# GpSimd waits for its cell scatters: a wait at every fourth scatter of a batch

## The reference

```python
loop = jnp.arange(n_nodes, dtype=edge_index.dtype)
row = jnp.concatenate([edge_index[0], loop])
col = jnp.concatenate([edge_index[1], loop])
deg = jax.ops.segment_sum(jnp.ones_like(col, dtype=jnp.float32), col, num_segments=n_nodes)
dinv = jnp.where(deg > 0, jax.lax.rsqrt(deg), 0.0)
norm = dinv[row] * dinv[col]
...
h = h @ W.T
msg = h[row] * norm[:, None]
out = jax.ops.segment_sum(msg, col, num_segments=n_nodes)
```

## The kernel before

| batch | block | scatters |
|---|---|---|
| 1 | end of attention, sums turned back tile by tile (`tiles`, line 1177) | 42 |
| 2 | normalize n1 | 17 |
| 3, 4, 5 | router of the two-expert layer, its choice, its weight loads | 6, 6, 9 |
| 6 | the two experts (`two_experts`, line 1972) | 135 |
| 7, 8 | normalize n2, n3 | 32, 24 |
| (none) | sum over edges: GpSimd gathers 416 tiles of rows | |
| 9, 10 | end of the sum, choice of the six-expert layer | 54, 5 |
| 11 | dispatch of rows to experts | 30 |
| singles | expert tiles: one before every second tile (line 2228) | 28 calls of one |
| 12 | collecting the expert rows (line 2419) | the last 28 |

## Time and profile before

### The profile page before, as it was taken

One profiled execution on the slowest core, in us unless ns is written; L12 is line 12 of the kernel. 1 busy time (PEld: TensorE's weight loads), 2 busy tenths in 40 slices (PEclk: granted clock), 3 DMA queues, 4 the chain that ended last, 5 costly groups with the idle time before them and its releaser, 6 DMA issues. The chain is left out here.

```text
span 5143.9 us, 62246 instructions
## 1 busy us (share of the span) xinstructions
PE 3848.2 (75%) x19117; PEld 2836.3 (55%) x19117; DVE 2174.4 (42%) x6089; ACT 1234.4 (24%) x3514; POOL 1935.0 (38%) x2021
## 2 busy tenths in 40 slices
PE   3877777234735555458399999996969999999597
PEld 2555555112425444357366665654538887777586
DVE  5555556600344444242300000005237777777723
ACT  3555454200100000012200000001125554444332
POOL 3455453474266666445400000001224444444053
PEclk8778888566866766668699999997579999999598
DMA  6655553000023333036454444443434444444266
GB/s 213 175 148 141 150 152 107 1 19 1 3 83 91 92 89 91 25 112 184 143 153 142 142 136 141 140 133 99 113 126 137 134 137 135 133 130 129 69 218 208
DMA packets 424073, 613.62 MB, mean 119 GB/s; under 512 B 149273, under 2 KB 287650, under 8 KB 423490
## 3 DMA queue, kind: packets, MB, share of 16 engines
q1 hardware_dynamic: 310578, 327.46, 22.2%
q0 software_dynamic: 104112, 273.76, 18.6%
q10 hardware_dynamic: 9056, 8.43, 0.5%
HBM read 517.83 MB, written 91.59 MB: 118 GB/s over the span
## 5 line engine op out<-in xcount | busy, mean ns | idle before, releaser
L2217 POOL DMA_INDIRECT stage<-t_row,f_take x168 | 162.1, 965 | 1269.7 <-POOLq L2064 1152.3
L865 POOL DMA_INDIRECT eg_rows<-t_edge,src_i x416 | 393.5, 946 | 563.7 <-DVE eg_pre L1698 422.1
L1108 PE MATMUL ps<-sum_hot,sum_rows 128*128 128x128 f32 x1664 | 330.0, 364 | 365.6 <-issue 201.5
L1372 PE MATMUL ps<-cv_cells,xn 128*128 128x384 f32 (+2 forms) x1600 | 535.7, 493 | 67.2 <-DMA cv_cells<-t_cells 67.2
L271 POOL DMA_INDIRECT t_cells<-times_seen,cell x416 | 409.8, 985 | 413.0 <-PEq L312 152.8
L865 POOL DMA_INDIRECT ag_rows<-t_att,src_i x416 | 401.7, 966 | 386.7 <-DVE ag_msg L970 264.6
L1108 PEld LDWEIGHTS ps<-sum_hot,sum_rows 128*128 128x128 f32 x1664 | 292.7, 264 | 403.0 <-issue 392.9
L865 POOL DMA_INDIRECT sum_rows<-t_row,src_i x416 | 393.9, 947 | 211.3 <-issue 116.5
L1050 PE MATMUL ps<-featT,ag_msg 128*128 128x128 f32 x1664 | 370.7, 357 | 127.2 <-issue 124.4
L1372 PEld LDWEIGHTS ps<-cv_cells,xn 128*128 128x128 f32 x1600 | 304.2, 190 | 279.5 <-DMA cv_cells<-t_cells 67.6
L1650 PE MATMUL ps<-eg_w,eg_rT 128*128 128x256 f32 x1664 | 439.3, 386 | 1.1 <-ACT eg_rT L1668 1.1
(11 more groups left out here) (418 smaller groups left out, 6296.4 us busy)
## 6 DMA issues: line engine op xcount, KB each, us to landing
cv_cells<-t_cells SPq DMA_DIRECT2D x225, 384.0 KB
cv_cells<-t_cells SPq DMA_DIRECT2D x75, 448.0 KB
xn<-in_L_ffn_W SPq DMA_DIRECT2D x57, 512.0 KB
t_cells<-zeros SPq DMA_DIRECT2D x17, 1664.0 KB
xn<-in_L_ffn_expert_w SPq DMA_DIRECT2D x110, 256.0 KB
ag_trow<-t_dst SPq DMA_DIRECT2D x104, 256.0 KB
t_cells<-zeros POOLq DMA_DIRECT2D x8, 1664.0 KB
eg_eaT<-in_edge_attr SPq DMA_DIRECT2D x208, 64.0 KB
```

What stands on the lines that cost most here:

```text
L865: nc.gpsimd.indirect_dma_start(out=rows[:, j, :], out_offset=None, in_=table, in_offset=bass.IndirectOffsetOnAxis(ap=src_i[:, n:n + 1], ax ...
L1108: mm = nc.tensor.matmul(ps[:, j % BANKS, k * EC:(k + 1) * EC], lhs, hot[:, j, :], start=True, stop=True)
L1372: mm = nc.tensor.matmul(ps[:, bank(q, k, half), 0:at.stop - at.start], source(l)[:, s, k * 128:(k + 1) * 128], cells[:, n % CR, at], start ...
L2217: nc.gpsimd.indirect_dma_start(out=xd[:, j, :], out_offset=None, in_=t_row, in_offset=bass.IndirectOffsetOnAxis(ap=take_row[:, n:n + 1], a ...
```

## The change

At every fourth scatter of a batch (offset 0, 4, 8, ... from the batch's first) GpSimd waits until `counted` stands at 16 for each scatter issued so far in the program. `seen[0]` is only raised at the end of a call, so the offsets start anew with each batch, and each of the 28 single calls has its one scatter at offset 0. Scatter 0 keeps its own two waits. Nothing else is changed; SUM_COUNTS, line 50, and the batches keep their sizes.

```diff
@@ -48,6 +48,7 @@
 EARLY_CLEARS = 8
 YR = 5
 SUM_COUNTS = 54
+PACE = 4
 
 
 class Signal:
@@ -268,6 +269,8 @@
             if c == 0:
                 pool.wait_ge(counted.sem, counted.at(0))
                 pool.wait_ge(g.cleared.sem, g.cleared.at(0))
+            elif (c - seen[0]) % PACE == 0:
+                pool.wait_ge(counted.sem, counted.at(16 * c))
             nc.gpsimd.indirect_dma_start(out=t_cells, out_offset=bass.IndirectOffsetOnAxis(ap=cell[:, c:c + 1], axis=0),
                                          in_=times_seen[:, c:c + 1], in_offset=None).then_inc(counted.sem, 16)
         seen[0] = min(RUN, seen[0] + many)
```

## The result

The changed kernel takes 4503.61 us (median of 4 runs, 4493.12 to 4532.5) beside 4390.77 us of the kernel before (4 runs, 4388.14 to 4394.56): ratio 1.0266, 95% interval 1.0236 to 1.0295. It is slower by 112.8 us; forecast were 84, in a range of 40 to 125. This holds for the chip that it was timed on.

The account below looks back on a forecast made before the run. Block by block, GpSimd arriving last at most scatter batches' ends was taken to bound the kernel. 84 waits x 1.1 us = 92.4, less 3.5 and 5 of slack, gave 84: 4390.4 + 84 = 4474 us, range 4430 to 4515.

Parts of the forecast that it names:

- What bounds: At block ends: GpSimd arrives last in timed runs in most scatter batches, 135 and 42 included, despite slack in the profile.
- Where the 753.5 us belong: Profiled span exceeds timed median by 753.5 us; mostly remote waits, taken as absent from timed runs with the slack they give.
- remote waits: VectorE waits whose releaser the profile calls "remote", with nothing at work behind them: 655.3 us in seven groups.
- 84 waits matter: Waits at offsets 4 and on inside batches, 84, cost time; those at offset 0 find scatters landed and cost nothing.
- 1.1 us a wait: Cost of each wait inside a batch for the fourth scatter's landing, bounded between 0.9 and 2.4 us; 84 make 92.4.
- Deductions 3.5 and 5: GpSimd slack taken off: 3.5 us in batches of 17, 54 and 5; 5 of 15.4 uncertain in 135 and 42.
- The last 28 hidden: Six waits in the last 28 scatters, about 7 us, fall inside 17 us of slack before the convolutions load.
- The batch of 32: Some scatters there take up to 2054 ns beside VectorE's work, so its 7 waits cost nearer 6 than 8 us.
- Covered: Rival: profile's slack is real in timed runs, only batches of 32, 24 and the small ones pay: 4408 us, 5%.
- Dear landing: Rival: a scatter's HBM receipt costs as much as a gather row's, 2.4 us a wait: 4583 us, 4%.
- the waits do nothing: Rival: a scatter has landed before the next would start, so time stays within 0.2%, 4390 us, 3%.
- The choke: Rival: scatters choke other engines; pacing ends half of 238.2 us of stall, 119 off and 84 on: 4355 us, 6%.

Follow-up runs that it names:

- experiment 4: Changed kernel with only the 39 waits at a batch's first scatter kept, on a chip with stalls: 5145.74 us, ratio 0.9995 to the kernel before.
- 2: Changed kernel with its waits put on a semaphore reached long before, so no scatter is waited for: 4390.34 us beside 4390.93 for the kernel before.
- second profile of before: The kernel before, profiled again with no edit: 4393.5 us, span 4391.8, no remote wait.
- experiment 6: Changed kernel with a wait at every eighth scatter instead of every fourth, on a chip with stalls: 5011.69 us, ratio 0.9737 to the kernel before.
- experiment 7: Changed kernel again with no edit, on another chip with stalls: 4959.92 us beside 5107.72 for the kernel before, ratio 0.9718.
- experiment 5: Changed kernel with groups of four on two semaphores in turn, each waiting for the group before the last: 5149.78 us, ratio 1.0001 to the kernel before.
- e_start: Changed kernel with waits at a batch's first scatter alone, none inside a batch: 5145.74 us beside 5147.69 for the kernel before, on a chip with stalls.
- a_again: The changed kernel, unedited, timed and profiled again on a chip with stalls: 4959.92 us, ratio 0.9718 to the kernel before.

## Why the prediction was right, and where it was not

**What bounds.** Right for the timed chip. GpSimd was last or level in the blocks of 42, 135, 32, 24 and 30, as the paces of the earlier trace rows said against the slack of the earlier trace rows; in the batch of 54 too, by its way out.

**Where the 753.5 us belong.** This step failed. I took the remote waits to belong to one profiled execution, and argued from it that they were absent from timed runs. They come with a chip: by the times they are present in all 34 runs of before on two chips and absent from its 41 on the others (4386 to 4433 us), with nothing in between. Each chip was used at one time only, so a state that it was in at that time isn't ruled out. That the forecast stands rests on the timed runs having been made on a chip without them; the timed 4390.4 said so for before, and that the changed kernel was timed on such a chip too was luck. But "the changed profile would still show the stall, near its size" was wrong: the changed kernel was profiled without any.

**84 waits matter.** Right: 84 and 6 more, 90 in all, none at an offset 0. Offset 0 costs nothing (experiment 4), the instruction neither (2).

**1.1 us a wait.** The mis-sized term. By batch, the 84 waits are 132.4 us of idle; less 84 x 0.30 that is 107.2, or 1.28 each. Most are at 1.12 to 1.13, near the 1.1 taken: it is 2.1 + 0.28 - 1.26 with the landing as now seen, where the earlier trace rows gave 1.9 and 0.9. But a few are long: 5.57 and 4.96 us in the blocks of 9 and 30, where the load queue is busy (all queues moved 232 GB/s in the 5 us ahead of the first, 225 in the 5.5 us around the second), and up to 3.4 near instruction-fetch packets. 107.2 - 92.4 = 14.8 us too few. The median of a landing isn't its price: a wait needs all of the landings before it, and pays the tail.

**Deductions 3.5 and 5.** 107.2 of waits became 100.3 of blocks, 6.9 less, beside 8.5. The places were different: nothing like the 5 us in 135 or 42; instead 2.9 in 42 (beside VectorE its scatters take 1065 ns on average in the second profile of before, 997 in the changed one, times 42), 1.7 in the batch of 17, 1.4 in 5, 0.8 in a batch of 6.

**The last 28 hidden.** Wrong by 6.4 us. The 17 us of slack came from the stalled profile; without stalls GpSimd ended at 1919.4 and the first load of the convolutions went out at 1929.53. The six waits took 16.5 us there, and the load goes out 2.6 us after GpSimd's end. The sum then is 84 + 14.8 + 1.6 (deducted too much) + 6.4 = 107, the span's difference. The timed medians differ by 6 us more, 112.8; the changed kernel's four runs lie 39 us apart (4493.12 to 4532.5), so this rest has no cause shown.

**The batch of 32.** By the Trainium skill, SBUF — State Buffer, the box on "DVE blocks DMA", its 7 waits were to cost nearer 6 than 8 us. The block grew by 8.3, and the waits were 1.43 us long on average: no discount was seen.

**The rivals.** Covered and Dear landing fell with the earlier trace rows and with the landing of 2.1 us; "the waits do nothing" with the 148.9 us. The choke got 6% and a price of half the stall. On the chip of the timing there was none. On a chip with stalls it was true, mechanism and sign: the stall in the blocks of the large batches is gone, 113 us of it in the block of 135, though not in the singles' stretch. My reason against it, that the rate only falls from one in 1.26 to one in 1.54 us, was no reason: at one in 1.40 us part of the stall is left (experiment 6), at one in 1.57 none (experiment 7), so the limit lies between.

**Open.** What fills. It is not unlanded scatters (in experiment 5 each wait found its landings in place, and the stall was whole), and not data (the DMA share is 0.01 to 0.02 in the block, on either kind of chip). The convolutions, with no GpSimd transfers, take 895 us on both kinds. TensorE's even pace of 1.40 us an instruction looks as if each instruction handed something on to a drain that it shares with the scatters; that is a guess. The Trainium skill, NOTIFIC — the notification-queue block, section 7.1, says that the block that writes an engine's trace records holds back its producers when its internal queues are full; that would fit, but no run here had the records off, so it isn't shown, and nor is why chips differ.

## What to carry to other kernels

When a profile's span is far from the timed median, find out whether the difference comes and goes from run to run or stays with the chip: time and profile the same kernel on the chip at hand before weighing any slack, and say of a result which kind of chip it holds for. A wait for what was just sent costs the landing that is left bare, and its tail; with two semaphores in turn no wait found anything missing. To rate-limit a sender, what matters is the rate, and where no neighbour is choked pacing is all price. That pacing only the choked blocks gains more where there are stalls was forecast and not seen.

## What was not expected of the hardware

- Chips differ, each as it was at its time: before took 4386 to 4395 us in 13 runs on one chip, 4390 to 4433 in 24 on two others, 5139 to 5158 in 27 on a fourth, 5095 to 5114 in 7 on a fifth.
- On the slower ones (seen in e_start and in the first profile of before) a stream of GpSimd scatters of 4 bytes a partition, one in 1.26 us, brings TensorE to one instruction in 1.40 us after 25 us; at one in 1.57 us it doesn't (a_again).
- A scatter's landing, 2.1 us, went up to 6.7.
- GpSimd needs a while to leave a block: from its last scatter's end to its sequencer's step at the barrier 1.49 us after a batch of 6, 2.15 after 135, 3.53 after 42, 4.51 after 54. In the block of 54 an engine that ended 4.1 us after it gave it no slack.
